# Perceiver layer, last layers: sixteen roots on ScalarE, two norms taken as one, FFN bias in the banks ahead, rounding offset on ScalarE

## The reference, cut to what matters

```
def group_rmsnorm_fused_gate(o, gate, w, num_heads):
    o = o * sigmoid(gate); og = o.reshape(b, n, num_heads, hd)
    og = og * rsqrt(mean(og * og, axis=-1, keepdims=True) + EPS)     # sixteen roots per row
    return og.reshape(b, n, d) * w
def bitlinear158(x, w, b):
    xq = act_quant(rms_norm(x))      # x * rsqrt(mean(x*x) + EPS), then 127 / max|x|, round, clip
    return einsum('bsd,od->bso', xq, weight_quant(w)) + b
h = silu(bitlinear158(_layernorm(x), w1, b1))     # a layer norm, and an rms norm of its result
h = layer_norm(gelu(h), ln_g, ln_b)               # inner width 2048
x = x + bitlinear158(h, w2, b2)
```

## Time and profile before

| | us |
|---|---|
| median of three runs (2004.03 to 2004.93) | 2004.54 |
| the profiled execution, device time | 2003.03 |
| its span | 2001.2 |
| of that, from the end of the cross attention's last value sum to the end | about 80 |

### The profile page before, as it was taken

The page is one execution under the profiler, slowest core; times in us unless marked ns, Lnnn a source line. Parts: engine busy times, 40 slices in busy tenths (PEclk is TensorE's granted clock), DMA queues, the critical chain, the costliest instruction groups (busy, mean ns, idle before and its releaser), DMA issues.

```text
span 2001.2 us, 46250 instructions
## 1 busy us (share of the span) xinstructions
PE 1944.2 (97%) x17334; PEld 1593.4 (80%) x17338; DVE 1606.9 (80%) x3444; ACT 1127.6 (56%) x2484; POOL 275.2 (14%) x465
## 2 busy tenths in 40 slices
PE   6899999999999999999999999999999999999896
PEld 5687987987887987977978977977978978877672
DVE  5788888888888888888888888888888888877736
ACT  4565666666656556556556565565565565655422
POOL 1011111111111111111111111111111111100001
PEclk8899999999999999999999999999999999999998
DMA  5678888887886887878878878887788787787470
GB/s 153 162 130 166 160 159 157 161 158 156 161 161 131 151 157 156 154 148 158 157 151 156 150 150 168 155 160 155 147 159 161 140 142 145 130 143 155 117 299 6
DMA packets 966944, 304.44 MB, mean 152 GB/s; under 512 B 893984, under 2 KB 952864, under 8 KB 965824
## 3 DMA queue, kind: packets, MB, share of 16 engines
q1 hardware_dynamic: 966720, 301.47, 76.6%
HBM read 72.16 MB, written 4.46 MB: 38 GB/s over the span
## 4 chain that ended last, share of the span: by engine, by line
PE 92%; DVE 5%; issue 1%; ACT 0%; DMA 0%; POOL 0%; SPq 0%; DVEq 0%; ACTq 0%; POOLq 0%
PE ps_v L1222 25%; PE ps_s L1207 25%; PE ps_t L1207 19%; PE ps_w L1222 19%; PE ps_v L1194 1%; PE ps_w L1181 1%; PE ps_v L1318 1%; DVE pp L887 1%; PE ps_t L1311 1%; PE ps_s L1161 0%; PE ps_s L1360 0%; DVE prob L882 0%; DVE bulk L835 0%; PE ps_v L1384 0%; DVE acc L896 0%
## 5 line engine op out<-in xcount | busy, mean ns | idle before, releaser
L1207 PE MATMUL ps_s<-bulk 128*128 128x128 f16 (+2 forms) x4752 | 583.0, 272 | 0.0
L1222 PE MATMUL ps_v<-nring,pt 128*128 128x256 f16 x4704 | 580.9, 273 | 1.6 <-ACT ps_w L651 0.9
L1222 PEld LDWEIGHTS ps_v<-nring,pt 128*128 128x128 f16 x4704 | 458.4, 98 | 62.1 <-DVE acc L806 2.6
L1207 PEld LDWEIGHTS ps_s<-bulk 128*128 128x128 f16 x4752 | 403.7, 98 | 111.9
L1207 PE MATMUL ps_t<-bulk 128*128 128x384 f16 (+2 forms) x3564 | 454.0, 272 | 13.9 <-ACT ps_t L665 8.4
L1222 PE MATMUL ps_w<-nring,pt 128*128 128x256 f16 x3528 | 451.9, 273 | 5.9 <-DVE ps_w L906 4.1
L887 DVE SCALAR_TENSOR_TENSOR pp<-prob,pp 128x384 f16<-128x384 f32 (+4 forms) x680 | 423.5, 690 | 0.0
L1207 PEld LDWEIGHTS ps_t<-bulk 128*128 128x128 f16 x3564 | 301.7, 98 | 106.6 <-ACT ps_t L665 9.5
L1222 PEld LDWEIGHTS ps_w<-nring,pt 128*128 128x128 f16 x3528 | 340.1, 98 | 54.8 <-DVE ps_w L906 6.4
L645 ACT ACTIVATE pp<-prob 128x384 f16<-128x384 f32 (+4 forms) x680 | 371.1, 624 | 7.8 <-DVE prob L882 6.8
L634 ACT ACTIVATE prob<-ps_s,nmax 128x768 f32<-128x768 f32 (+2 forms) x136 | 119.1, 876 | 431.1 <-DVE nmax L862 425.8
(11 more groups left out here) (187 smaller groups left out, 1400.8 us busy)
## 6 DMA issues: line engine op xcount, KB each, us to landing
stage<-in_ctx SPq DMA_DIRECT2D x196, 128.0 KB, 2.8
wst<-in_w SPq DMA_DIRECT2D x64, 256.0 KB, 3.1
bulk<-in_vo SPq DMA_DIRECT2D x16, 512.0 KB, 6.3
acc<-in_qk SPq DMA_DIRECT2D x11, 512.0 KB, 4.3
pt<-pp SPq DMA_TRANSPOSE x272, 5.6
tern_d<-wter SPq DMA_DIRECT2D x32, 128.0 KB, 2.9
bulk<-tern_d SPq DMA_DIRECT2D x2, 2048.0 KB, 20.3
nring<-in_aw SPq DMA_DIRECT2D x3, 1024.0 KB, 11.1
```

Of the source, the lines that this page charges most:

```text
L1207: ins = mm(out if n == 1 else out.rearrange("p (n m) -> p n m", m=P), q_part(e, qlo, a)[:, c * P:(c + 1) * P], t_moving(k, run, tlo, b, c) ...
L1222: ins = mm(dst, pt[:, tile:tile + P], n_part(c, clo, b), start=(first and n == 0 and plo == 0 and clo == 0), stop=(last and n == w - 1 and ...
```

## The change

- Roots: DVE adds a reciprocal of the sixteen values (128x16), ACT takes a `Sqrt` of it in place of POOL's power; `refine` waits for ACT. ACT names `Sqrt` on one element ahead and `Gelu` on one element behind (two table loads where one stood).
- Two norms as one: the variance is scaled by (1 + EPS) plus EPS squared and one inverse root serves both norms. The first statistics read `ps_c` itself, and so does the subtraction of the mean; ACT's copy of x2 follows them. The maximum of |y| is taken ahead of `refine`.
- Bias: DVE computes 1/factor and factor/2, waits for the transposes (`f_tp`), and writes b1/factor into the four banks; L1416 accumulates on top, each bank behind its `h_seed`. `h_in` is gone: tanh and silu read the banks, the tanh (behind all four seeds) and the gelu take the scale from a column in memory.
- Rounding: DVE does two of the three steps of each quarter; ACT subtracts the offset (`h_round`), then the transposes. DVE copies the last two of the four transposed quarters.
- PE: the scores go e outside, j inside; `keep_warm(28)` becomes 20 over four banks; `keep_warm(2)` stands behind two of the transposes.

```diff
+            nc.scalar.activation(rl[0:1, 0:1], ident[0:1, 0:1], ACT.Sqrt)
+            act.wait_ge(ms_inv, 1)
+            nc.scalar.activation(ms[:, 2 * AH:3 * AH], ms[:, 3 * AH:4 * AH], ACT.Sqrt).then_inc(ms_root, 1)
+            nc.scalar.activation(rl[0:1, 1:2], mhalf[0:1, 0:1], ACT.Gelu)
...
-            act.wait_ge(ap_mm, 1)
+            act.wait_ge(x2_read, 1)
             nc.scalar.activation(x2[:, :], ps_c[:, :], ACT.Copy).then_inc(x2_done, 1)
...
-                act.wait_ge(h_done, n + 1)
-                nc.scalar.activation(slot(8 + n), slot(n), ACT.Tanh, scale=0.5).then_inc(h_exp, 1)
+                act.wait_ge(h_mm, n + 1)
+                act.wait_ge(h_seed, 4)
+                nc.scalar.activation(slot(8 + n), h_bank(n), ACT.Tanh, scale=st[:, 50:51]).then_inc(h_exp, 1)
...
-                nc.scalar.activation(slot(4 + n), slot(8 + n), ACT.Gelu, scale=0.5).then_inc(h_gelu, 1)
+                nc.scalar.activation(slot(4 + n), slot(8 + n), ACT.Gelu, scale=st[:, 50:51]).then_inc(h_gelu, 1)
...
-            for n in range(4):
+            def h_round(n):
+                act.wait_ge(f2_q, n + 1)
+                nc.scalar.activation(h_bits(n), slot(n), ACT.Copy, bias=-MAGIC).then_inc(f2_b, 1)
+            h_round(0)
+            h_round(1)
+            for n in range(2):
                 act.wait_ge(f2_tp, n + 1)
-                nc.scalar.activation(h_rows_t(n), h_turned(n),
-                                     ACT.Copy).then_inc(f2_tc, 1)
+                nc.scalar.activation(h_rows_t(n), h_turned(n), ACT.Copy).then_inc(f2_tc[0], 1)
+                h_round(n + 2)
...
-            nc.vector.tensor_scalar(ms[:, AH:2 * AH], ms[:, 0:AH], 0.25 / AHD, EPS, ALU.mult, ALU.add).then_inc(lnx, 1)
+            link(nc.vector.tensor_scalar(ms[:, AH:2 * AH], ms[:, 0:AH], 0.25 / AHD, EPS, ALU.mult, ALU.add))
+            nc.vector.reciprocal(ms[:, 3 * AH:4 * AH], ms[:, AH:2 * AH]).then_inc(ms_inv, 1)
...
-            link(nc.vector.bn_stats(st[:, 0:6], x2[:, :]))
+            v.wait_ge(ap_mm, 1)
+            link(nc.vector.bn_stats(st[:, 0:6], ps_c[:, :]))
             link(nc.vector.bn_aggr(st[:, 6:8], st[:, 0:6]))
-            nc.vector.tensor_scalar(st[:, 8:9], st[:, 7:8], EPS, None, ALU.add).then_inc(lnx, 1)
-            link(nc.vector.tensor_scalar(y, x2[:, :], st[:, 6:7], None, ALU.subtract))
+            nc.vector.tensor_scalar(st[:, 8:9], st[:, 7:8], 1.0 + EPS, EPS * EPS, ALU.mult, ALU.add).then_inc(lnx, 1)
+            nc.vector.tensor_scalar(y, ps_c[:, :], st[:, 6:7], None, ALU.subtract).then_inc(x2_read, 1)
+            v.wait_ge(x2_read, 1)
+            link(nc.vector.tensor_reduce(st[:, 17:18], y, AX.X, ALU.max, apply_absolute_value=True))
             refine(st[:, 9:10], st[:, 8:9], st[:, 10:11])
-
-            link(nc.vector.scalar_tensor_tensor(st[:, 12:13], st[:, 9:10], st[:, 7:8], st[:, 9:10], ALU.mult, ALU.mult))
-            nc.vector.tensor_scalar(st[:, 12:13], st[:, 12:13], EPS, None, ALU.add).then_inc(lnx, 1)
-            link(nc.vector.tensor_reduce(st[:, 17:18], y, AX.X, ALU.max, apply_absolute_value=True))
-            row_factors(0, True)
+            row_factors(st[:, 9:10])
...
+            link(nc.vector.reciprocal(st[:, 51:52], st[:, 19:20]))
+            link(nc.vector.tensor_scalar(st[:, 50:51], st[:, 19:20], 0.5, None, ALU.mult))
+            v.wait_ge(f_tp, 1)
+            for n in range(4):
+                nc.vector.tensor_scalar(h_bank(n), b1b[:, n * D:(n + 1) * D], st[:, 51:52], None, ALU.mult).then_inc(h_seed, 1)
...
-                nc.vector.scalar_tensor_tensor(slot(8 + n), slot(8 + n), 1.0, slot(n), ALU.add,
+                nc.vector.scalar_tensor_tensor(slot(8 + n), slot(8 + n), 1.0, h_bank(n), ALU.add,
...
             link(nc.vector.tensor_tensor(slot(14), x2[:, :], b2b, ALU.add))
+            for n in (2, 3):
+                v.wait_ge(f2_tp, n + 1)
+                nc.vector.tensor_copy(h_rows_t(n), h_turned(n)).then_inc(f2_tc[1], 1)
...
-            for j in range(4):
-                dst = (ps_s, ps_s, ps_t, ps_t)[j]
-                for e in range(4):
+            for e in range(4):
+                for j in range(4):
...
-                last.then_inc(sc_mm, 1)
+                    if e == 3:
+                        last.then_inc(sc_mm, 1)
...
             transposes(ps_t, slot(14), KC, ident).then_inc(at_mm, 1)
+            keep_warm(2, ps_s[:, 0:D])
...
-            keep_warm(28)
+            keep_warm(20, h_bank(0), h_bank(1), h_bank(2), h_bank(3))
...
+            keep_warm(2, ps_b)
             pe.wait_ge(f_tc, 1)
...
+                pe.wait_ge(h_seed, n + 1)
                 for c in range(KC):
...
+                    last = mm(h_bank(n), rows_t[:, c * P:(c + 1) * P], tern[:, c * F + n * D:c * F + (n + 1) * D],
+                              start=False, stop=(c == KC - 1), skip_group_check=True)
```

More of the change, by code:

```diff
@@ L224, in h_turned, with h_bank, h_bits @@
             return (ps_t, ps_s)[n // 2][:, (n % 2) * D:(n % 2) * D + D // 2].bitcast(BF16)
+        def h_bank(n):
+            return (ps_s, ps_t)[n // 2][:, (n % 2) * D:(n % 2 + 1) * D]
+        def h_bits(n):
+            return slot(12 + n // 2)[:, (n % 2) * D // 2:(n % 2 + 1) * D // 2].bitcast(BF16)
         def cols(k):
@@ L369, in perceiver_layer @@
         f2_tp = sem("f2_tp")
-        f2_tc = sem("f2_tc")
+        f2_tc = [sem(f"f2_tc{g}") for g in range(2)]
         f2_mm = sem("f2_mm")
@@ L588, in _ @@
             rsqrt_guess(2, st[:, 9:10], st[:, 8:9], 1)
[L589 to L592, removed]
+            rsqrt_guess(3, st[:, 9:10], st[:, 8:9], 1)
+            rsqrt_guess(4, st[:, 9:10], st[:, 8:9], 1)
+            rsqrt_guess(5, st[:, 13:14], st[:, 12:13], 1)
         @block.scalar
@@ L1059, in _, with row_factors @@
                                     ALU.mult).then_inc(an_done, 1)
[L1060 to L1070, removed]
+            def row_factors(f):
                 link(nc.vector.tensor_scalar(st[:, 17:18], st[:, 17:18], f, 1e-5, ALU.mult, ALU.max))
@@ L1073, in row_factors, with to_8_bits @@
                 link(nc.vector.tensor_scalar(st[:, 18:19], st[:, 18:19], 127.0, f, ALU.mult, ALU.mult))
-            def to_8_bits(y, dst, ready):
+            def to_8_bits(y):
                 link(nc.vector.tensor_scalar(y, y, st[:, 18:19], MAGIC, ALU.mult, ALU.add))
-                link(nc.vector.tensor_scalar(y, y, MAGIC + 127.0, MAGIC - 128.0, ALU.min, ALU.max))
-                nc.vector.tensor_scalar(dst, y, -MAGIC, None, ALU.add).then_inc(ready, 1)
+                return nc.vector.tensor_scalar(y, y, MAGIC + 127.0, MAGIC - 128.0, ALU.min, ALU.max)
             def back_factor(w):
@@ L1095, in _ @@
-            link(nc.vector.tensor_reduce(st[:, 17:18], y, AX.X, ALU.max, apply_absolute_value=True))
-            row_factors(0, True)
-            to_8_bits(y, slot(2)[:, 0:D // 2].bitcast(BF16), f_q)
-            back_factor(0)
-            def h_in(n):
-                v.wait_ge(h_mm, n + 1)
-                src = (ps_s[:, 0:D], ps_s[:, D:2 * D], ps_t[:, 0:D], ps_t[:, D:2 * D])[n]
-                nc.vector.scalar_tensor_tensor(slot(n), src, st[:, 19:20], b1b[:, n * D:(n + 1) * D], ALU.mult,
-                                               ALU.add).then_inc(h_done, 1)
+            row_factors(st[:, 9:10])
@@ new lines, in _ @@
+            link(to_8_bits(y))
+            nc.vector.tensor_scalar(slot(2)[:, 0:D // 2].bitcast(BF16), y, -MAGIC, None, ALU.add).then_inc(f_q, 1)
+            back_factor(0)
+            link(nc.vector.reciprocal(st[:, 51:52], st[:, 19:20]))
[3 more added lines that the diff above has]
+                nc.vector.tensor_scalar(h_bank(n), b1b[:, n * D:(n + 1) * D], st[:, 51:52], None, ALU.mult).then_inc(h_seed, 1)
@@ L1339, in _, with keep_warm @@
             add_out(H - 1)
-            def keep_warm(n):
-                for _ in range(n):
-                    mm(ps_s[:, 0:D], identb[:, :], wter[:, 0:D], start=True, stop=True)
-            keep_warm(14)
+            def keep_warm(n, *banks):
+                for i in range(n):
+                    mm(banks[i % len(banks)], identb[:, :], wter[:, 0:D], start=True, stop=True)
+            keep_warm(14, ps_s[:, 0:D])
             pe.wait_ge(ydone, 2)
@@ L1387, in _ @@
             mm(ps_c[:, :], ident[:, :], x1[:, :], start=True, stop=False)
-            keep_warm(16)
+            keep_warm(16, ps_s[:, 0:D])
             pe.wait_ge(an_done, 1)
             transposes(ps_t, slot(14), KC, ident).then_inc(at_mm, 1)
+            keep_warm(2, ps_s[:, 0:D])
             pe.wait_ge(at_cp, 1)
@@ L1399, in second @@
             def second(n):
-                pe.wait_ge(f2_tc, n + 1)
+                pe.wait_ge(f2_tc[n // 2], n % 2 + 1)
                 for k in range(4):
@@ L1413, in _ @@
             for n in range(4):
+                pe.wait_ge(h_seed, n + 1)
                 for c in range(KC):
-                    dst = (ps_s, ps_s, ps_t, ps_t)[n]
```

(11 more changed lines are left out.)

24 lines of the change are left out of this document (13 added, 11 removed).

## The result

The changed kernel takes 1994.74 us in the median of six runs (1993.26 to 1996.41), the kernel before 2005.01 in six (2004.03 to 2006.20): a ratio of 0.9949 with an interval of 0.9938 to 0.9960, some 10 us. Ten more runs of it, in two later comparisons, gave ratios of 0.9954 (0.9941 to 0.9967) and 0.9964 (0.9951 to 0.9976); over all sixteen the mean is 1995.7, against 2004.6 for 86 runs of the kernel before, so 8.9 us (one more run of it, of 2054.33, belongs to the chip's slow state and is left out). The forecast was 2000.2, a gain of 4.3, in a range that ended at 1997.9: the direction was right, the size was less than half of the 10.3 of the medians and about half of the 8.9 of the means.

The account below looks back on a forecast made before the run. PE's cross attention, left alone, was taken to bound the kernel; in the last 80 us, gains of 0.48 + 0.4 + 2.25 + 0.8 + 0.35 = 4.3 took the median 2004.54 to 2000.2 us, range 1997.9 to 2002.3.

Parts of the forecast that it names:

- (b): First quantisation, from the end of the output product to `f_q`: 5.29 us in place of 7.55, a gain of 2.25.
- (c): Inner part of the FFN, from `f_q` to the last `bn_stats`: bias written ahead gains 0.8 us, from 0.6 to 1.7.
- (d): Second quantisation, first L1077 to L1151: rounding on ACT gains 0.35 us, from -0.2 to 0.8.
- rival 2: FFN seeds are written at the memory rate: gain 5.2 us, 1999.3; chance 0.14.
- rivals 3 and 4: Scores don't overlap in the new order: gain 2.8, chance 0.12; second quantisation gives nothing back: gain 3.7, chance 0.07.
- rival 5: Clock falls ahead of the output product and first FFN product: slower by 2.8 us, 2007.3; chance 0.05.
- (a): Linear attention: roots gain 2.65 us on DVE, 0.48 on the path; the order of the scores gains 0.4.
- if the clock falls at the same instant: Condition in (a) for time won in the scores' order counting double in L1384, steps 0.11 or 0.21 us apart.
- rival 1: Keep-warm matmuls ahead of the linear attention's transposes don't bind, roots worth 2.65: gain 6.5 us, 1998.0; chance 0.12.
- four at a time: Upper bound for the scores' overlap in the new order: L1384 starts 0.9 us earlier; 0.4 was taken.

Follow-up runs that it names:

- before_scores_roots: The kernel before with both the new order of the scores and the roots by ScalarE: 2000.21 us, ratio 0.9982.
- after_warm4: The kernel after with four keep-warm matmuls between the scores and the values' product: 1995.17 us, ratio 0.9956.
- before_warm4: The kernel before, old order of the scores, with four keep-warm matmuls between the scores and the values' product: 2003.03 us, ratio 0.9995.
- after_scores_back: The kernel after with the old order of the scores (j outside): 1999.16 us, ratio 0.9970.
- before_scores: The kernel before with the new order of the scores alone (e outside, j inside): 2004.04 us, ratio 1.0000.
- before_roots: The kernel before with the sixteen roots by ScalarE alone (reciprocal on DVE, Sqrt, table loads): 2002.11 us, ratio 0.9988.

## Why the prediction was wrong

- **(b), (c), (d) held.** 2.24 for 2.25, 0.61 for 0.8, 0.54 for 0.35. The subtraction out of the bank took 0.74 (forecast 0.75), the seeds 0.75 (0.75), tanh and gelu 0.68 and 0.72 (0.69, 0.72); the seeds in a bank cost the slower price, so rival 2 fell; the scores overlap and (d) gave its gain, so rivals 3 and 4 fell too, and the clock beneath both products of rival 5 stayed up. The row behind 0.69 for the tanh (L634) has its column as a bias, not as a scale as I read it; the measured 0.68 bears the price out all the same. DVE's copies of the bf16 quarters took 0.42 where I had 0.69 at most; they can be but a small part of the surplus of (d), since the first multiply already stood 3.01 us behind the first L1094 for the 3.1 forecast, and the rest took 4.11 for 4.2. The groups of after by line and shape:

```profile
L1119 DVE TENSOR_SCALAR ps_s<-bulk,st 128x512 f32<-128x512 f32 x2 | 1.4, 749 | 0.1
...
L1165 DVE COPY prob<-ps_s 128x512 bf16<-128x512 bf16 x2 | 0.8, 424 | 0.6 <-PE ps_s L1177 0.6
...
L1107 DVE TENSOR_SCALAR acc<-ps_w,st 128x512 f32<-128x512 f32 x1 | 0.7, 740 | 0.0
```

- **(a) failed: 0.9 forecast, 4.5 in the profile, 4.3 by the means of before_scores_roots.** What I named as late next, the sixteen keep-warm matmuls, was right: they hold the transposes behind DVE's last step by 0.9 to 1.5 us in every profile with sixteen of them and the roots on ScalarE, except that of after_warm4, whose clock stayed up all through (0.06). Wrong was their price. The step that failed is "if the clock falls at the same instant" and, for the keep-warm matmuls, the 0.50 of one window, which I took as given for the kernel after. With the old order the values' product took 6.0, 6.15, 6.29, 6.76, 6.69 and 3.79 us in six profiles (mean 5.9); with the new one 3.73 in seven and 4.00, 5.31, 5.36 and 5.68 in four (mean 4.2). (before_warm4 is left out of the six, since four dense matmuls stand ahead of its product; after_warm4, one of the seven, has them too.) The low stretch begins early in the product with the old order, mostly, and late or behind it with the new. That also shortens it for the keep-warm matmuls, which now held PE back by only 0.9 us, so that the roots were worth 1.8 of their 2.65 in place of 0.48. I had this as rival 1 with 0.12, and priced it with the roots alone; its true size is the roots' part plus the 2.0 in the product.
- **The order of the scores: four at a time.** Rows of after show two `ps_s` and two `ps_t` instructions every 0.11 us, all 32 within 1.2 us: the upper end of my bounds. The start of the values' product moved by 0.65, between the ends, since DVE takes its first bank no earlier than before (1943.07 is 14.28 us behind the gate product, 1941.80 was 14.27): the first bank is now ready with the last. That the new order leaves the clock up more often rests on the profiles and on the time of after_scores_back; the time and the mean clock of before_scores don't bear it out. Why it would isn't shown; before_warm4, with dense matmuls at that place, is a hint at the density and no more.
- **Missing from the sum: the clock beneath the first FFN product.** Rival 5 looked for it in the kernel after. It was in the kernel before: of six profiled kernels with the old first quantisation and 28 keep-warm matmuls, five ran that product low (10.6 to 11.0 us to the last `bn_stats`), and the one that didn't (9.3) is the one I read. None of the ten with the new quantisation and at least twenty keep-warm matmuls did. So the change also takes away some 1.3 us that my profile didn't contain (an estimate: 10.6 to 11.0 against 9.3, in five of six). It is also part of why that profile stood 1.5 us below the median of its own kernel, a difference that the prediction stated and then carried along unexplained.
- **The sum again:** 4.5 + 1.3 + 2.24 + 0.6 + 0.54 = 9.2, against 8.9 by the means. The 10.3 of the first medians is within the spread of that. So close an agreement is partly luck: 4.5 is the difference of two single executions.
- **What stays open.** How much of (a) is the order itself and how much a chance of the profiles taken: eleven profiles against six is a clear lean, no proof of the mean, and before_scores, 0.4 us for the 3 that its profile promised, speaks against it. And whether trimming the remaining waits gains anything.

## What to carry to other kernels

Where PE's clock is low in a stretch of the profile, don't carry that stretch over to the changed kernel: it can be the state of one execution, so price every PE-bound term at both levels and let the difference set the range. Read a profiled execution that stands below its kernel's median as a warning that it lacks a cost that others have, and look for the PE work behind idle stretches that could have run low. Where two releases meet at one wait, removing one is worth no more than the distance to the other: test them alone and together.

## What the runs showed of the hardware

- Four 32-row groups, each with its own PSUM bank, advanced together: 32 instructions of 32x128 f32 in 1.2 us, 0.11 per step of all four, against 2.8 us when issued group by group. The earlier trace had shown two together, and starts out of program order at the seam.
- PE's clock differs from execution to execution of one program: 80 runs of the kernel before have mean granted clocks of 0.986 to 0.992. The same old-order product took 3.79 us in before_roots and 6.69 in after_scores_back. An idle stretch of at most 1.04 us ahead of the FFN's transposes left it at 2.4 GHz in all eleven profiles with one, one of 1.55 to 1.8 us was followed by 1.2 GHz in five of six, one of 2.76 in its one.
- Added work made a kernel no slower: seven more matmuls (1.5 us of PE) took 1.8 us off by the means; the ratio's interval, 0.9983 to 1.0000, just reaches no change.
- A table switch on ScalarE cost its 1.28 us row and nothing behind it that shows: the load ends at 1952.19, and the one-element gelu starts at 1952.20.
